# Scores of four heads in row tiles of 32, straight from the split queries, in a cross-attention kernel on Trainium2

## What is computed

```python
# x: (16, 512, 512), context: (16, 77, 512), 16 heads of 32
Q = split_heads(query @ Wq + bq)
K = split_heads(key @ Wk + bk)
V = split_heads(value @ Wv + bv)
scores = jnp.einsum('bhqd,bhkd->bhqk', Q, K) / np.sqrt(D_K).astype(np.float32)
attn = jax.nn.softmax(scores, axis=-1)
ctx = jnp.einsum('bhqk,bhkd->bhqd', attn, V)
ctx = ctx.transpose(0, 2, 1, 3).reshape(B, S, D_MODEL)
out = ctx @ Wo + bo
return _layer_norm(out + query, ln_gamma, ln_beta)
```

## Time and profile before

| | us |
|---|---|
| median of 3 runs | 677.35 |
| lowest, highest | 676.78, 677.64 |
| profiled execution, its own time | 677.69 |
| its span | 675.9 |
| PE busy, share of the span | 643.8, 95% |
| DVE busy | 555.0, 82% |
| POOL busy | 453.7, 67% |
| ACT busy | 319.7, 47% |
| DMA packets, share of 16 engines | 71.8% |

### The profile page before, as it was taken

The page is one execution under the profiler, slowest core; times in us unless marked ns, Lnnn a source line. Parts: engine busy times, 40 slices in busy tenths (PEclk is TensorE's granted clock), DMA queues, the critical chain, the costliest instruction groups (busy, mean ns, idle before and its releaser), DMA issues.

```text
span 675.9 us, 11503 instructions
## 1 busy us (share of the span) xinstructions
PE 643.8 (95%) x3336; PEld 435.1 (64%) x3336; DVE 555.0 (82%) x842; ACT 319.7 (47%) x547; POOL 453.7 (67%) x396
## 2 busy tenths in 40 slices
PE   6989997999999999999999999999999999999990
PEld 5978754666666666666666666666666666665570
DVE  5534484888889898888988888889888888988986
ACT  5612254545545555554555545455554544544431
POOL 0422143477777777777787777777877777666897
PEclk9999996999999999999999999999999999999996
DMA  9757788767776868778787778686767778675512
GB/s 318 288 198 186 193 203 208 179 162 199 194 201 170 209 180 205 204 195 215 201 197 184 201 186 204 190 201 186 198 177 206 198 205 215 152 185 154 162 62 93
DMA packets 105677, 129.55 MB, mean 192 GB/s; under 512 B 49936, under 2 KB 49936, under 8 KB 105648
## 3 DMA queue, kind: packets, MB, share of 16 engines
q1 hardware_dynamic: 105648, 129.19, 71.8%
HBM read 53.94 MB, written 24.35 MB: 116 GB/s over the span
## 4 chain that ended last, share of the span: by engine, by line
PE 77%; DVE 6%; SPq 6%; issue 2%; POOL 1%; DMA 1%; ACT 0%; POOLq 0%; DVEq 0%; ACTq 0%
PE p_q L584 24%; PE p_o L646 23%; PE p_s L614 9%; PE p_v L627 9%; PE p_d L630 7%; PE p_a L600 5%; SPq L519 3%; DVE rden L799 2%; SPq L505 1%; DMA xt<-in_x_t 1%; DVE cxt L813 1%; DVE stats L795 1%; DVE y L793 0%; POOL rstd L932 0%; DVE stats L887 0%
## 5 line engine op out<-in xcount | busy, mean ns | idle before, releaser
L799 DVE RECIPROCAL rden<-p_d 128x512 f32<-128x512 f32 x64 | 214.9, 3358 | 27.8 <-PE p_d L630 27.7
L709 ACT ACTIVATE prob<-p_s 77x512 f32<-77x512 f32 x256 | 144.0, 588 | 111.4 <-PE p_s L614 111.0
L834 DVE TENSOR_REDUCE nm<-p_a 128x4 f32<-128x308 f32 x256 | 117.4, 462 | 29.3 <-PE p_a L600 26.0
L936 POOL TENSOR_TENSOR y<-y,gamma_row 128x512 f32<-128x512 f32 x60 | 76.7, 1278 | 70.7 <-ACT y L739 70.7
L926 POOL TENSOR_TENSOR xl<-xt,xh 128x512 fp32r<-128x512 f32 x60 | 77.5, 1291 | 64.8 <-ACT xh L716 63.5
L584 PE MATMUL p_q<-xh,wqh 128*128 128x512 f32 x256 | 101.8, 398 | 1.7 <-PEq L148 1.7
L584 PE MATMUL p_q<-xl,wqh 128*128 128x512 f32 x256 | 101.8, 398 | 0.0
L584 PE MATMUL p_q<-xh,wql 128*128 128x512 f32 x256 | 101.1, 395 | 0.0
L945 POOL TENSOR_TENSOR cl<-cxt,ch 128x512 fp32r<-128x512 f32 x64 | 82.5, 1288 | 26.3 <-ACT ch L734 26.3
L739 ACT ACTIVATE y<-y,nmr,rstd 128x512 f32<-128x512 f32 x60 | 48.9, 815 | 106.1 <-DVE nmr L818 106.1
L614 PE MATMUL p_s<-z,ks 97*77 97x512 f32 x256 | 95.7, 414 | 0.0
(11 more groups left out here) (114 smaller groups left out, 911.8 us busy)
## 6 DMA issues: line engine op xcount, KB each, us to landing
z<-qh SPq DMA_DIRECT2D x256, 128.0 KB, 2.7
xt<-in_x_t SPq DMA_DIRECT2D x64, 256.0 KB, 2.8
z<-ql SPq DMA_DIRECT2D x128, 128.0 KB, 2.4
xn<-in_x SPq DMA_DIRECT2D x60, 256.0 KB, 3.1
out_dram<-y SPq DMA_DIRECT2D x60, 256.0 KB, 3.3
ks<-k_high SPq DMA_DIRECT2D x32, 154.0 KB, 3.5
cx<-in_ctx_t SPq DMA_DIRECT2D x4, 616.0 KB, 5.4
k_high<-kth SPq DMA_DIRECT2D x4, 616.0 KB, 3.5
```

What stands on the lines that cost most here:

```text
L709: nc.scalar.activation(prob[0:S2, j, :], p_s[j % 2][0:S2, :], ACT.Exp, scale=SCALE).then_inc(prob_ready, 1)
L799: nc.vector.reciprocal(rden[:], p_d[:]).then_inc(rden_ready, 1)
L834: nc.vector.tensor_reduce(nm[:, t, HC * (g.k % 2):HC * (g.k % 2 + 1)], p_a[t % 2][:, 0:HC * S2].rearrange("p (h k) -> p h k", k=S2), AX_X, ...
```

## The change

The operands z and ks go. Each head's scores are four matmuls on a row tile: head j of the chunk lies on partitions 32j to 32j+31 of qh and ql already, so `tile_position=(32j, 0)` places its matmul on the array's rows 32j to 32j+31. The four parts (k_high by qh, k_low by qh, k_high by ql, and a one-row matmul of ones by the maxima) are summed in the head's own PSUM bank. The keys are loaded as two operands kch and kcl, the maxima into mrow, one partition for each head, by 8 DMAs for a pair of groups where there were 4. The 12 copies of z go. There are four banks p_s and none p_a: `rowmax_scores` writes into the same four banks, one for each 128 queries, so each waits for the exp of the same slot that empties its bank, and the slot's scores wait for the four maxima of the slot before. All 16 matmuls of the scores stand at the slot's start. exp 3 comes ahead of q_high in every slot. Only p_q is free early for `project_last`, the three other banks not until the last exps.

```diff
-        z = sb("z", [P, 2, HALF, S], F32R)
-
-        ks = sb("ks", [P, 2, NCH * HC, S2], F32R)
+        mrow = sb("mrow", [P, 2, 2, S], F32R)
+        ones_row = sb("ones_row", [P, S2], F32R)
+
+        kch, kcl = (sb(n, [P, 2, NCH, S2], F32R) for n in ("kch", "kcl"))
...
-        p_s = [psum(f"p_s{i}") for i in range(2)]
-        p_a = [psum(f"p_a{i}") for i in range(2)]
+        p_s = [psum(f"p_s{i}") for i in range(HC)]
...
-        last_banks = [(p_q, ql_ready, NG), (p_a[0], max_ready, NG * QT), (p_a[1], max_ready, NG * QT),
-                      (p_s[0], prob_ready, NG * HC)]
+        last_banks = [(p_q, ql_ready, NG)] + [(p_s[j], prob_ready, (NG - 1) * HC + j + 1) for j in range(QT - 1)]
...
-                for part, src in enumerate((kh_dram, kl_dram, kh_dram)):
-                    sp.dma_start(ks[DK * part:DK * (part + 1), i, :, :].bitcast(F32),
-                                 src[b.over(NCH)].rearrange("(h d) k -> d h k", d=DK)).then_inc(ks_in[i], 16)
+                for dst, src in ((kch, kh_dram), (kcl, kl_dram)):
+                    sp.dma_start(dst[:, i, :, :].bitcast(F32),
+                                 src[b.over(NCH)].rearrange("(c p) k -> p c k", p=P)).then_inc(ks_in[i], 16)
...
-                all_at_least(sp, (max_turned, c.over(2, 1)))
...
+                all_at_least(sp, (max_turned, c.over(2, 1)), (s_summed, c.over(2, -1, HALF)))
                 for b in range(P // DK):
-                    sp.dma_start(row[:, :, :, b, :], nmt[DK * b:DK * b + HALF, i, :, :]).then_inc(mx_in[i], 16)
+                    for cc in range(2):
+                        rows_of = mrow[0:P:DK, i, cc, :].bitcast(F32).rearrange("h (t b r) -> h t b r", t=QT, r=DK)
+                        at = DK * b + HC * cc
+                        sp.dma_start(rows_of[:, :, b, :], nmt[at:at + HC, i, :, :]).then_inc(mx_in[i], 16)
...
-                    for part, src in enumerate((qh, qh, ql)):
-                        for j in range(HC):
-                            sp.dma_start(z[DK * part:DK * (part + 1), i, j::HC, :].bitcast(F32),
-                                         src[DK * j:DK * (j + 1), i, :, :].bitcast(F32)).then_inc(z_in[i], 16)
...
+                at_least(pe, prob_ready, g.over(1, -LAG_AS, HC) + t + 1)
+                nc.tensor.matmul(p_s[t][:, 0:HC * S2], qh[:, g.k // 2 % 2, g.k % 2, P * t:P * (t + 1)],
                                  kb[g.k // NCH % 2][:, g.k % NCH, :], start=True, stop=True).then_inc(a_summed, 1)
...
-                at_least(pe, prob_ready, g.over(1, 0, HC) + j - 1)
-                nc.tensor.matmul(p_s[j % 2][0:S2, :], ks[0:KR, g.k // NCH % 2, h, :], z[0:KR, i, s, :],
-                                 start=True, stop=True).then_inc(s_summed, 1)
...
+                at_least(pe, prob_ready, g.over(1, 0, HC))
+                ahead = g.over(1, LAG_AS, QT)
+                at_least(pe, max_ready, min(ahead, QT * NG) if isinstance(ahead, int) else ahead)
+
+                def row_tile(part, j):
+                    h = slice(DK * j, DK * (j + 1))
+                    one = slice(DK * j, DK * j + 1)
+                    k, q = ((kch[h, b, c, :], qh[h, i, cc, :]), (kcl[h, b, c, :], qh[h, i, cc, :]),
+                            (kch[h, b, c, :], ql[h, i, cc, :]), (ones_row[one, :], mrow[one, i, cc, :]))[part]
+                    return nc.tensor.matmul(p_s[j][0:S2, :], k, q, start=(part == 0), stop=(part == 3),
+                                            tile_position=(DK * j, 0))
+                for part in range(3):
+                    for j in range(HC):
+                        row_tile(part, j)
+                for j in range(HC):
+                    row_tile(3, j).then_inc(s_summed, 1)
...
-                steps = [(t, c) for t in range(QT - 1)]
+                steps = [(0, c)]
                 if c >= NCH - 2:
-                    steps += [(QT - 1, kc) for kc in (range(NCH - 1) if c == NCH - 2 else (c,))]
+                    steps += [(t, kc) for t in range(1, QT) for kc in (range(NCH - 1) if c == NCH - 2 else (c,))]
...
-                    scores_after, maxima_after = (1, 3), (2, 4, 5, 6)
+                    maxima_after = (2, 4, 5, 6)
...
-                if g.k % 2 == 0:
-                    at_least(act, z_in[i], g.over(4, 0, 16 * Z_DMAS))
+                at_least(act, s_summed, g.over(1, -3, HC))
```

More of the change, by code:

```diff
@@ L372, in attend @@
         wo_in = [sem(f"wo_in{i}") for i in range(2)]
-        z_in = [sem(f"z_in{i}") for i in range(2)]
         mx_in = [sem(f"mx_in{i}") for i in range(2)]
@@ L594, in rowmax_scores @@
                         pe.wait_ge(kb_in[g.k // NCH % 2], g.over(PAIR, 1, 16 * KB_DMAS))
[L596 to L600, removed]
-                                 kb[g.k // NCH % 2][:, g.k % NCH, :], start=True, stop=True).then_inc(a_summed, 1)
@@ new lines, in rowmax_scores, with scores @@
+                nc.tensor.matmul(p_s[t][:, 0:HC * S2], qh[:, g.k // 2 % 2, g.k % 2, P * t:P * (t + 1)],
+                                 kb[g.k // NCH % 2][:, g.k % NCH, :], start=True, stop=True).then_inc(a_summed, 1)
+            def scores(g):
+                i, cc, b, c = g.k // 2 % 2, g.k % 2, g.k // NCH % 2, g.k % NCH
+                if g.is_first():
+                    pe.wait_ge(const_dve, 2)
+                pe.wait_ge(qh_ready, g.over(1, 1))
+                pe.wait_ge(ql_ready, g.over(1, 1))
+                pe.wait_ge(mx_in[i], g.over(4, 1, 16 * MX_DMAS))
+                if c == 0:
+                    pe.wait_ge(ks_in[b], g.over(PAIR, 1, 16 * KS_DMAS))
+                at_least(pe, prob_ready, g.over(1, 0, HC))
[13 more added lines that the diff above has]
+                    row_tile(3, j).then_inc(s_summed, 1)
@@ L672, in slot @@
                 if s.valid(NG):
-                    scores(s, 0)
-                    scores(s, 1)
+                    scores(s)
                 parts = [(project_q, q, kc) for kc in range(KC) if q.valid(NG)]
@@ L679, in slot @@
                 if len(parts) == 2 * KC:
-                    scores_after, maxima_after = (1, 3), (2, 4, 5, 6)
+                    maxima_after = (2, 4, 5, 6)
                 elif s.valid(NG):
-                    scores_after, maxima_after = (0, 1), (1, 2, 3, 3)
+                    maxima_after = (1, 2, 3, 3)
                 else:
-                    scores_after, maxima_after = (), (0, 1, 2, 3)
+                    maxima_after = (0, 1, 2, 3)
                 for n, (project, chunk, kc) in enumerate(parts):
                     project(chunk, kc)
-                    for j, after in enumerate(scores_after):
-                        if s.valid(NG) and after == n:
-                            scores(s, 2 + j)
                     for t, after in enumerate(maxima_after):
@@ L708, in exp @@
                     at_least(act, pv_summed, g.over(1))
-                nc.scalar.activation(prob[0:S2, j, :], p_s[j % 2][0:S2, :], ACT.Exp, scale=SCALE).then_inc(prob_ready, 1)
+                nc.scalar.activation(prob[0:S2, j, :], p_s[j][0:S2, :], ACT.Exp, scale=SCALE).then_inc(prob_ready, 1)
             def split_x_high(n):
@@ L747, in _ @@
             act.wait_ge(keep["bq_in"], 16)
-            def is_short(g):
-                return not g.back(LAG_OUT).valid(NS) or not g.valid(NG)
             def slot(g):
                 s, v, m, n = g.back(LAG_SCORE), g.back(LAG_PV), g.back(LAG_NORM), g.back(LAG_SPLIT)
-                short = is_short(g)
                 if s.valid(NG):
@@ L762, in slot @@
                     exp(s, 2)
-                if s.valid(NG) and short:
+                if s.valid(NG):
                     exp(s, 3)
@@ L766, in slot @@
                     q_high(g)
-                if s.valid(NG) and not short:
-                    exp(s, 3)
                 if v.valid(NG):
@@ L782, in _ @@
             nc.vector.memset(nm[:], 0.0).then_inc(const_dve, 1)
-            nc.vector.memset(ks[QI:KR, :, :, :].bitcast(F32), 1.0).then_inc(const_dve, 1)
+            nc.vector.memset(ones_row[:].bitcast(F32), 1.0).then_inc(const_dve, 1)
             dve.wait_ge(const_dve, 2)
@@ L823, in q_low @@
                 dve.wait_ge(qh_ready, g.over(1, 1))
-                if g.k % 2 == 0:
-                    at_least(dve, z_in[i], g.over(4, 0, 16 * Z_DMAS))
+                at_least(dve, s_summed, g.over(1, -3, HC))
                 nc.vector.scalar_tensor_tensor(
```

8 lines of the change are left out of this document (3 added, 5 removed).

## The result

| | before | after |
|---|---|---|
| median of 4 runs, us | 677.34 | 681.98 |
| lowest, highest | 676.78, 677.64 | 681.88, 682.39 |
| profiled execution, its own time | 677.69 | 681.97 |
| its span | 675.9 | 680.2 |

The changed kernel takes 1.0081 times as long (95% interval 1.0067 to 1.0094): slower by 0.8%. The forecast was 676.0.

A forecast was written before the change was run, and what follows sets the result against it. PE's own time was taken to bound the steady part and SP's queue the start. Profiled 677.69 - 8.8 (start) + 5.5 (steady) + 1.9 (end) = 676.3, less 0.34 for the median: 676.0 us; range 670.5 to 694.

The forecast's parts named there:

- likeliest case: Whole kernel: near-full overlap of row tiles, +0.05 to +0.15 us a slot, 673.2 to 678.7 us; chance 0.45.
- What bounds the kernel: Steady part: PE's own time, 9.075 us per slot; start: SP's queue, with copies of z 28% of the chain.
- Four row tiles side by side: Score block in full slots: near-full overlap, lower bound 0.93 us as before; without overlap 3.72 us.
- Rival B: Score block: row-tile loads in series or partly hidden, +0.2 to +0.45 us a slot, 681.5 to 695 us; chance 0.25.
- Rival C: Score block: PE fed too slowly, 721 us, or tiles not side by side, 824 us; chance 0.08.
- The change of tiling: Full slots: one change more at 0.07 us, plus 0.03 for tiles starting and signalling in turn; +5.5 us over 55 slots.
- break-even: Head against steady part: they nearly cancel, so from +0.125 us a slot on the change is a loss.
- Rival D: Full slots: third change of tiling free, 0 to +0.03 us a slot, 670.5 to 672 us; chance 0.12.
- Waits in the full slot costed at nothing: Full slots: new waits of maxima, scores, q_high and xt are covered, maxima by 1.5 us or more; cost nothing.
- The start: Slots 5 to 8: without SP's 12 copies per pair, DVE bounds at 6.80 us a slot; -8.8 us taken.
- rival E: Start gives half because maxima land after the scores want them: -4 us there, 677.5 to 683 us; chance 0.10.
- The end: `project_last`: 12 more matmuls in slot 68 delay DVE's add by +1.9 us; what follows on DVE stays as it stands.

The follow-up runs named there:

- e5_full_rows: Changed kernel with its 16 row-tile matmuls replaced by four full 128-row ones, without low parts and maxima; order, banks, waits and DMAs kept: 669.99 us.
- e3_copies_back: Changed kernel with the 12 copies of qh and ql per pair of groups issued on SP again, into a buffer nobody reads: 693.95 us.
- e2_no_max_part: Changed kernel without the fourth, one-row part of the scores, so the maxima are made and copied but not subtracted: 668.37 us.
- e1_two_blocks: Changed kernel with the row tiles in two visits, parts 2 and 3 moved behind p_q's first three matmuls: 704.45 us.
- e6_full_between: Changed kernel with the row-tile block moved behind p_q's first three matmuls, so column and row tiles don't touch: 694.15 us.

## Why the prediction was wrong

The time lay in the range, but beyond the likeliest case's 673 to 679, and on the other side of no change. Step by step:

**What bounds the kernel: right.** PE's own time is the steady part's, SP's queue, or what it carries, the start's. e5_full_rows shows the one, e3_copies_back the other.

**Four row tiles side by side: right, near the lower bound as taken.** Parts start 0.23 us apart, and e2_no_max_part puts one at 0.236. Rival B's mechanism, loads in series, is refuted by the loads that start within 0.02 us, although its band of 681.5 to 695 holds the measured 681.98, and +0.197 lies at the edge of its +0.2: nearly the right price for a wrong reason. Loads do stand bare, but one at each change of tiling, and none within the block. Rival C, a block fed too slowly, is refuted by the same rows. The Trainium skill (TensorE: Matmul & The Clock Gate, Part 3: Packing small matmuls) reports 3.07 times for four row tiles. Inside the stream the trace doesn't agree: it is 0.23 us for four, 4.0 times. For the block with its edge to p_q it is 16 x 0.232 = 3.72 over 308.39 - 307.31 = 1.08 us, 3.4 times.

**The change of tiling: wrong, and this is the failed step.** The prediction said: "The changed slot has one change more (columns to rows, rows to full), between 0.05 and 0.10; I take 0.07, and 0.03 for four tiles that start and signal one behind another." Measured are 0.06 at the way in and 0.10 + 0.11 at the way out, 0.27, less the 0.055 of before: 0.21 by the edges, 0.197 by the slots. A change of tiling costs two things that add up: a gap (0.10 to 0.11), and the first load behind it, which isn't hidden and costs by its columns, 77 at about 0.06 and 128 at 0.11. So the third change costs 0.21 where I took 0.07. I had the 0.10 of the way into the columns and the 0.055 of the way out, read them as two prices of one thing and took a value between them. The gap of the way out was in the trace of before too, but I counted it as the values' own time: 1.86 us as four passes of 0.465, where the groups start 0.43 apart and the last step is 0.54. With both gaps read, and the two loads' sizes of the earlier trace rows, 0.10 + 0.11 + 0.06 - 0.055 = 0.215 could have been worked out, +11.8 us for 55 slots and 682.3 in all. That four tiles start and signal one behind another cost nothing: the parts stand a pass apart, and e1_two_blocks has the same step out with signals and without. e1_two_blocks and e6_full_between pay the edges again, at the sizes expected.

The break-even, "from +0.125 us a slot on the change is a loss", was right, and 0.197 is above it. Rival D, a free third change, falls.

**Waits in the full slot costed at nothing: right.** PE has no idle time from 200 to 400, and e5_full_rows, with the same order and waits, has slots of 9.065.

**The start: right.** -8.71 for -8.8, slots of 6.85 bound by DVE, no lower clock. The maxima arrive in time, so rival E falls. "The chain through 44 to 125 us is made of SP's issues" says too much: they add up to 47% of it, its largest part, and how much of the gain is owed to less traffic in the DMA engines stays open. The first block of row tiles, in slot 4, before the slots that I counted, was left out of the sum.

**The end: right in its term, short behind it.** DVE's add is +1.90 later for +1.9 predicted; "What follows on DVE I take as it stands" missed the 0.68 that POOL's wait gives back.

In the sum, the failed step is +5.3 us (10.8 for 5.5); slot 4 and the head +1.0, the end -0.7, the start +0.1. That is 5.7 of the 5.98 us between 676.0 and 681.98; the rest is, within 0.1, the 0.34 between the profiled execution of before and its median, which the one of after doesn't have.

## What to carry to other kernels

A visit to another tiling of the array costs at its edges, not by its work: at each change a gap of about 0.1 us and one bare weight load of the next size, and the two add. Count the edges in the order of PE's program, price each from the nearest edge in the trace with its own load, look for the gap inside blocks too, by the starts of their groups, and gather tiled matmuls in one block next to another tiled one. And before replacing work to relieve a queue, move what is waited for to its front: in the profiled executions two lines in SP's order won a third of what the whole rewrite won in the start, at no cost on PE.

## What the runs showed of the hardware that was not expected

Weights of four row tiles load side by side, within 0.02 us (77 columns), and four such matmuls run at the pitch of one, 0.23 us. At a change of tiling the next load starts only when the new block does: bare for 0.06 us at 77 columns and 0.11 to 0.12 at 128. Beside it there was a gap of 0.09 to 0.11 us at every change in these traces: full to columns, columns to full, columns to rows, full to rows, rows to full. And twice the DMA traffic, a share of 0.72 for 0.34, did not change PE's slot of 9.272 us by a hundredth.
